# Group mean, values and FFN moved ahead of the query product on TensorE, and the copies issued ahead of the image's load

## The reference

```python
x = x + bn(dwconv(x, dw0_w, 1), dw0_bn)             # x: the image after a group norm (32 groups)
x = ffn(x, ffn0_w1, ffn0_bn1, ffn0_w2, ffn0_bn2)    # x + pw(relu(pw(x)))
x = x + window_attn(x, qkv_w, qkv_bn, qdw_w, qdw_bn, attn_bias, proj_w, proj_bn)
x = x + bn(dwconv(x, dw1_w, 1), dw1_bn)
x = ffn(x, ffn1_w1, ffn1_bn1, ffn1_w2, ffn1_bn2)
...
# window_attn: 25 windows of 7x7 (padded at two edges), 4 heads, 16 channels for queries and keys, 32 for values
q = bn(dwconv(q, qdw_w, 2), qdw_bn)                  # 5x5 depthwise convolution of the queries, per window
attn = softmax(einsum('bhcn,bhcm->bhnm', q, k) * KD ** -0.5 + bias)
out = einsum('bhdm,bhnm->bhdn', v, attn)
return pw(relu(out), proj_w, proj_bn)
```

## Time and profile before

| | before |
|---|---|
| median of 3 runs | 4045.66 us (4044.58 to 4047.29) |
| the profiled execution's own time | 4038.97 us |
| its span, first to last instruction | 4037.1 us |
| TensorE matmul busy | 3184.8 us (79%) |
| VectorE busy | 2720.9 us (67%) |
| ScalarE busy | 2203.4 us (55%) |
| mean granted TensorE clock | 0.889 of full speed |

### The profile page before, as it was taken

The page is one execution under the profiler, slowest core; times in us unless marked ns, Lnnn a source line. Parts: engine busy times, 40 slices in busy tenths (PEclk is TensorE's granted clock), DMA queues, the critical chain, the costliest instruction groups (busy, mean ns, idle before and its releaser), DMA issues. The chain is left out here.

```text
span 4037.1 us, 80272 instructions
## 1 busy us (share of the span) xinstructions
PE 3184.8 (79%) x29652; PEld 2441.9 (60%) x29652; DVE 2720.9 (67%) x5162; ACT 2203.4 (55%) x3568; POOL 743.2 (18%) x869
## 2 busy tenths in 40 slices
PE   4787878787846658888888888888888886699993
PEld 2444445454535546767766777676767675587872
DVE  4767676767544448777777777777777775577763
ACT  2444454545524437666666666666656663477760
POOL 1000000000000000122122121121221122466660
PEclk9898999999967779989899888899889997899995
DMA  2344444445437689999999999999999994577768
GB/s 55 108 159 115 155 118 152 122 148 164 131 134 271 246 285 375 342 333 343 345 352 347 329 346 332 347 351 336 337 337 336 366 334 151 187 243 236 242 201 334
DMA packets 291012, 1023.89 MB, mean 254 GB/s; under 512 B 51620, under 2 KB 57520, under 8 KB 281574
## 3 DMA queue, kind: packets, MB, share of 16 engines
q1 hardware_dynamic: 273382, 985.62, 70.5%
q0 software_dynamic: 17280, 33.87, 2.3%
HBM read 486.25 MB, written 489.85 MB: 242 GB/s over the span
## 5 line engine op out<-in xcount | busy, mean ns | idle before, releaser
L1094 DVE CUSTOM_DVE_ANT_0 att_skewed<-att_score_ps,att_skewed 128x1024 f32<-128x1024 f32 x512 | 625.2, 1221 | 260.1 <-issue 243.2
L956 ACT ACTIVATE att_skewed<-att_skewed,att_neg_max 128x1024 f32<-128x1024 f32 x512 | 588.8, 1150 | 347.9 <-DVE att_neg_max L1094 347.0
L1212 PE MATMUL att_turn_ps<-att_ident,att_skewed 128*128 128x128 f32 x4096 | 592.0, 291 | 112.7 <-ACT att_skewed L956 110.4
L947 ACT ACTIVATE att_rows<-att_wide_ps 128x1152 f32<-128x1152 f32 x512 | 574.1, 1121 | 176.3 <-PE att_wide_ps L1176 174.9
L1212 PEld LDWEIGHTS att_turn_ps<-att_ident,att_skewed 128*128 128x128 f32 x4096 | 494.7, 149 | 280.3 <-ACT att_skewed L956 242.1
L1102 DVE COPY att_turned<-att_turn_ps 128x1024 f32<-128x1024 f32 x512 | 625.0, 1221 | 27.7 <-PE att_turn_ps L1212 27.4
L1176 PE MATMUL att_wide_ps<-att_ps,att_qs 98*128 98x128 f32 (+3 forms) x1920 | 452.9, 359 | 53.9 <-issue 29.6
L1204 PE MATMUL att_score_ps<-att_ks,att_qs 96*128 96x512 f32 x1024 | 379.7, 454 | 19.4 <-DVE att_neg_max L1094 17.9
L911 POOL DMA_INDIRECT expert_rows<-att_expert_rows,att_place x256 | 247.1, 965 | 786.6 <-DVE att_place L1052 701.2
L1176 PEld LDWEIGHTS att_wide_ps<-att_ps,att_qs 98*128 98x128 f32 x1920 | 324.5, 209 | 109.2 <-issue 67.7
L152 POOL DMA_INDIRECT expert_parts<-exp_parts,exp_rows x284 | 301.4, 1061 | 192.3 <-ACT exp_parts L183 126.3
(11 more groups left out here) (257 smaller groups left out, 5586.5 us busy)
## 6 DMA issues: line engine op xcount, KB each, us to landing
skewed_rows<-att_rows SPq DMA_DIRECT2D x512, 576.0 KB, 5.5
att_skewed<-skewed_rows SPq DMA_DIRECT2D x512, 512.0 KB, 6.9
expert_rows<-conv_pad SPq DMA_DIRECT2D x144, 520.0 KB, 10.9
exp_weights<-split_weights SPq DMA_DIRECT2D x71, 1028.0 KB, 7.0
att_qs<-queries SPq DMA_DIRECT2D x192, 128.0 KB
att_ks<-keys SPq DMA_DIRECT2D x192, 128.0 KB
exp_rows<-expert_rows SPq DMA_DIRECT2D x71, 260.0 KB, 2.8
sum_part<-expert_parts SPq DMA_DIRECT2D x32, 512.0 KB, 9.6
```

The source lines that it names most:

```text
L947: act.activation(rows[s % ROWS][:], wide_ps[:, 0:WIDE], ACT.Copy).then_inc(wide_read, 1)
L956: act.activation(skewed[r % RING][:], skewed[r % RING][:], ACT.Exp, bias=neg_max[:, k:k + 1], scale=-1.0, accum_out=sums[:, k:k + 1]).then ...
L1094: dve.tensor_tensor_reduce(skewed[r % RING][:], score_ps[:], skewed[r % RING][:], -SCALE, 3.0e38, ALU.add, ALU.min, neg_max[:, k:k + 1]).t ...
L1212: last = pe.transpose(turn_ps[:, t * P:(t + 1) * P], skewed[r % RING][:, t * P:(t + 1) * P], ident[:])
```

## The change

On TensorE the turn becomes: scores, group mean, first part of the values, first half of FFN 1 (both hidden halves), second part of the values, FFN 1's output, queries, transposes and the rest as before. Of the convolution's four chunks the fourth goes between the hidden halves and the output of FFN 0. The tile rotation (`main_items`, `first_items`) follows this order. ScalarE's order is adapted: values, relu, first exponential, relu, values, windows, second exponential, queries; and the fourth chunk of the convolution is read after FFN 0's relus. On SyncE `copies(n + 1)` comes ahead of the wait for `xp_ready` and the load of image n + 3. VectorE's and GpSimd's programs keep their order; of VectorE's only the tiles differ.

```diff
-        main_items = [*((item, 0) for item in S_ITEMS + ["V0", "V1"]), ("Q", 1), ("G", 2), *((item, -1) for item in F1),
-                      *((item, 0) for item in T_ITEMS + ["A0", "A1", "P0", "P1"]), *((item, 1) for item in ["K0", "K1"] + C_ITEMS),
-                      *((item, 2) for item in F0)]
+        main_items = [*((item, 0) for item in S_ITEMS), ("G", 2), ("V0", 0), ("F1a", -1), ("F1b", -1), ("V1", 0), ("F1c", -1), ("Q", 1),
+                      *((item, 0) for item in T_ITEMS + ["A0", "A1", "P0", "P1"]), *((item, 1) for item in ["K0", "K1"] + C_ITEMS[:3]),
+                      ("F0a", 2), ("F0b", 2), ("C3", 1), ("F0c", 2)]
...
             def turn(n):
+                if not is_last(n):
+                    copies(n + 1)
                 if not (isinstance(n, int) and n >= NB - 3):
                     sp.wait_ge(xp_ready, n + 3)
                     sp.dma_start(x[:], x_dram[n + 3]).then_inc(x_loaded, 16)
-                if not is_last(n):
-                    copies(n + 1)
...
             def turn(n):
...
+                values_of(n, 0)
+                if not is_first(n):
+                    ffn(n - 1, 1, y, "a")
+                exponentials(n, 0)
+                if not is_first(n):
+                    ffn(n - 1, 1, y, "b")
+                values_of(n, 1)
                 if not is_last(n):
                     into_windows(n + 1)
-                exponentials(n, 0)
+                exponentials(n, 1)
                 if not is_last(n):
                     queries(n + 1)
-                exponentials(n, 1)
                 if not is_first(n):
-                    ffn1(n - 1)
+                    filled(act, place(n - 1, "F1c"))
...
                     keys_of(n + 1)
-                    convolved(n + 1)
+                    convolved(n + 1, (0, 1, 2))
                     keep_branch(n + 1)
                 if has_after_next(n):
                     ffn0(n + 2)
+                if not is_last(n):
+                    convolved(n + 1, (3,))
...
+            def prepare(n):
+                convolution(n, (0, 1, 2))
+                if not is_last(n):
+                    pe.wait_ge(x1_ready, n + 2)
+                    ffn_in(n + 1, 0, x1)
+                convolution(n, (3,))
+                if not is_last(n):
+                    ffn_out(n + 1, 0)
...
             def turn(n):
...
+                if has_after_next(n):
+                    moments_mean(n + 2)
+                values_of(n, 0)
+                if not is_first(n):
+                    pe.wait_ge(x4_ready, n)
+                    ffn_in(n - 1, 1, x4)
+                values_of(n, 1)
+                if not is_first(n):
+                    ffn_out(n - 1, 1)
                 if not is_last(n):
                     queries(n + 1)
-                if has_after_next(n):
-                    moments_mean(n + 2)
-                if not is_first(n):
-                    ffn1(n - 1)
...
                 if not is_last(n):
                     keys_of(n + 1)
-                    convolution(n + 1)
-                if has_after_next(n):
-                    ffn0(n + 2)
+                    prepare(n + 1)
```

More of the change, by code:

```diff
@@ L1538, in ffn0, with values_of @@
                 ffn(n, 0, branch, "ab")
-            def ffn1(n):
-                ffn(n, 1, y, "ab")
-                filled(act, place(n, "F1c"))
+            def values_of(n, v):
+                at = place(n, f"V{v}")
+                filled(act, at)
+                first, k = 16 * v, min(16, WINDOWS - 16 * v)
+                for low in range(2):
+                    rows = slice(64 * low, 64 * low + WIN)
+                    source = tile[at[0]][rows, 0:k * 64].rearrange("p (w a d) -> p w a d", w=k, a=2)
+                    ins = act.activation(values[rows, first:first + k, :, low * DH:(low + 1) * DH], source, ACT.Copy)
+                ins.then_inc(tile_used[at[0]], 1)
             def queries(n):
@@ L1561, in keys_of, with convolved @@
                                        last=(h == HEADS - 1 and s > 0))
-            def convolved(n):
-                for j in range(4):
+            def convolved(n, chunks):
+                for j in chunks:
                     at = place(n, f"C{j}")
@@ L1623, in prologue @@
                 keys_of(0)
-                convolved(0)
+                convolved(0, (0, 1, 2))
                 keep_branch(0)
                 ffn0(1)
-            image_loop(act, prologue, turn, lambda: ffn1(NB - 1))
+                convolved(0, (3,))
+            image_loop(act, prologue, turn, lambda: ffn(NB - 1, 1, y, "ab"))
         @block.vector
@@ L1834, in begin, with ffn_in @@
                 return tile[where[0]]
-            def ffn(n, number, source):
+            def ffn_in(n, number, source):
                 for j in range(2):
@@ L1842, in ffn, with ffn_out @@
                     last.then_inc(tile_filled[at[0]], 1)
+            def ffn_out(n, number):
                 at = place(n, f"F{number}c")
@@ L1889, in keys_of, with convolution @@
                     last.then_inc(tile_filled[at[0]], 1)
-            def convolution(n):
-                pe.wait_ge(copied, 256 * n + 256)
-                for j in range(4):
+            def convolution(n, chunks):
+                if 0 in chunks:
+                    pe.wait_ge(copied, 256 * n + 256)
+                for j in chunks:
                     at = place(n, f"C{j}")
@@ L1907, in prologue, with values_of @@
                 moments_mean(1)
-                ffn0(0)
+                pe.wait_ge(x1_ready, 1)
+                ffn_in(0, 0, x1)
+                ffn_out(0, 0)
                 queries(0)
                 keys_of(0)
-                convolution(0)
-                ffn0(1)
+                prepare(0)
+            def prepare(n):
[6 more added lines that the diff above has]
+                    ffn_out(n + 1, 0)
+            def values_of(n, v):
+                at = place(n, f"V{v}")
+                to = begin(at)
+                for j in range(min(16, WINDOWS - 16 * v)):
+                    for low in range(2):
+                        last = pe.matmul(to[64 * low:64 * low + WIN, 64 * j:64 * j + 64], xw[:, 16 * v + j, :], w_v[:, low, :], start=True, stop=True)
+                last.then_inc(tile_filled[at[0]], 1)
             def turn(n):
@@ L1929, in turn @@
                     last.then_inc(tile_filled[at[0]], 1)
[L1930 to L1934, removed]
-                            last = pe.matmul(to[64 * low:64 * low + WIN, 64 * j:64 * j + 64], xw[:, 16 * v + j, :], w_v[:, low, :], start=True, stop=True)
-                    last.then_inc(tile_filled[at[0]], 1)
+                if has_after_next(n):
[7 more added lines that the diff above has]
+                    ffn_out(n - 1, 1)
                 if not is_last(n):
                     queries(n + 1)
-                if has_after_next(n):
-                    moments_mean(n + 2)
-                if not is_first(n):
-                    ffn1(n - 1)
                 for j in range(4):
@@ L1973, in turn, with epilogue @@
                     keys_of(n + 1)
-                    convolution(n + 1)
-                if has_after_next(n):
-                    ffn0(n + 2)
-            image_loop(pe, prologue, turn, lambda: ffn1(NB - 1))
+                    prepare(n + 1)
+            def epilogue():
+                pe.wait_ge(x4_ready, NB)
+                ffn_in(NB - 1, 1, x4)
+                ffn_out(NB - 1, 1)
+            image_loop(pe, prologue, turn, epilogue)
 def tables():
```

17 lines of the change are left out of this document (1 added, 16 removed).

## The result

The changed kernel takes **3936.36 us** (median of 4 runs, 3928.71 to 3939.22), the kernel before 4045.12 us in runs beside it: the ratio is 0.9733, 95% interval 0.9711 to 0.9756. The profiled execution took 3937.88 us with a span of 3935.8. Forecast were 3924 us and a range of 3895 to 3975.

What follows compares the result with a forecast made beforehand. TensorE's order with two late suppliers bounds each turn. Turns 0 to 12 give 113 us, turn 13 1.2, turns 14 and 15 3 each, prologue 0.9: 121 us, so 3918 profiled, 3924 as median; range 3895 to 3975.

Steps and rivals of the forecast that it cites:

- Two late suppliers: On TensorE, the convolution waits for its copies and the query product for the windows, 4.5 to 5 us each turn.
- The first half: Scores to keys on TensorE: queries follow at once and warm, attention starts at 27.1, keys end at 36.8.
- the wait of the values: On TensorE, the values' second part waits 1.8 us for VectorE's copy that releases the group mean's tile.
- the transposes' wait: On TensorE, the third transposes wait 3.1 us, until 24.5, for VectorE to read the FFN's output tile.
- The clock: TensorE's clock falls behind the transposes' 3.1 us wait, costing 1.2 us a turn, bounds 0 and 9.
- Rival 2: Clock falls at the new waits, staying low through attention, projection and keys: 5 us a turn, 3977 us; chance 0.10.
- rival 1: Clock stays high past the 3.1 us wait: turn 57.1 us, bound by copies, 3910 us in all; chance 0.22.
- The copies: On SyncE, issued at 20.7 and landed 15.1 us later at 35.8, just covered; the load behind costs nothing.
- Turn 0: First turn of the convolution phase: said to wait like turns 1 to 12 and to gain the same 8.7 us.
- The exponential between the relus: On ScalarE, the first exponential takes 1.53 us, to 11.9; one table load in the whole phase was noted.
- The second half: Convolution start to next scores takes 21.2 us; the relu wait shrinks from 1.39 to about 0.5 us.
- rival 3: The new TensorE order gains nothing and only the copies help: 98 us gained, 3948 us; chance 0.15.

Runs made afterwards that it cites:

- e1: The kernel before with only SyncE's copies moved ahead of the image's wait and load, old engine order kept: 3956.29 us, ratio 0.9787 to the kernel before.
- e2: The changed kernel with SyncE's old order, the image's load ahead of the copies: 3950.94 us, ratio 0.9774 to the kernel before.
- e10: e3 plus a fourth unread matmul behind the last transposes, in the wait for ScalarE's copy: 3909.34 us, ratio 0.9670 to the kernel before.
- e5: The changed kernel with VectorE's sum moved into a softmax gap and the tile's read ahead of the group norm: 3906.28 us, ratio 0.9669 to the kernel before.
- e9: The program of e3 run once more, unedited, beside the changed kernel: 3923.47 us, ratio 0.9699 to the kernel before.
- e7: e5 with VectorE's copy of the group mean ahead of the two maxima: 3899.37 us, ratio 0.9656 to the kernel before.
- e6: The changed kernel with VectorE's group norm moved behind the sum and the read: 3917.89 us, ratio 0.9696 to the kernel before.
- e3: The changed kernel with three unread matmuls on TensorE filling the wait before the third group of transposes: 3933.26 us, ratio 0.9729 to the kernel before.

## Why the prediction was right, and where it was off

**The bound.** Two late suppliers to an ordered TensorE: right. Each, removed alone (e1, e2), gives most of the gain.

**The first half.** In turn 7 the wait of the values was 1.48 us (1.8 forecast); the queries followed at 17.0 (17.2), warm; the transposes' wait was 3.37 us (3.1) and ended at 24.4 (24.5). The new order's effect was right to 0.3 us at each step.

**The clock.** This is the term that was mis-sized. The direction was right, a fall behind the 3.1 us wait, but I priced it at 1.2 us. With the clock kept high (e10) a turn takes 56.78 us, so the fall costs 2.3 us: in the turn shown the transposes and nearly the whole attention ran at half rate, and the clock rose only with the projection. On average over turns 1 to 12 the attention started at 27.7 (27.1 forecast) and the convolution at 38.0 (36.8). In turn 1 the attention started at 28.2, beyond the 28 that the prediction gave as a sign of being wrong. Rival 2 named the mechanism with 5 us a turn and rival 1 its absence; at 57.1 us a turn rival 1's time was 0.3 from what e10 shows. That the low clock comes every turn was the Trainium skill's reading (TensorE: Matmul & The Clock Gate, HAM oscillation): the trace of the changed kernel agrees in turns 1 to 14, but e5 and e9 have turns with equal waits where it comes and where it doesn't.

**The copies.** In turns 1 to 13 issued at 20.6 (20.7), landed before the keys' end, no wait: right. That 15.1 us from issue to start is the price with nothing ahead is shown by e5 and e7 from turn 2 on. The load behind them cost nothing: no engine waited for it. Turn 0 was wrong. The prediction gave it the gain of the other turns, but its copies took 16.65 us and the convolution waited 4.89 us for them.

**The exponential between the relus.** It loads no table: the changed kernel's trace has one table load in this phase, at 44.2 us, as before, and none in a turn. The query product was due at 17.2 and came at 17.0.

**The second half.** From the convolution at 552.34 to the scores at 573.38 it took 21.0 us, forecast 21.2; the relu's wait was 0.22 us, not 0.5.

**The sum.** Forecast 121 us, found 106.0 in the phase: turns 1 to 12 gave 12 x 7.73 = 92.8 instead of 104; turn 0 5.1 instead of 8.7 (its turn is 60.9 us; e1's is 57.6, where the copies are issued at 16.7 and the convolution doesn't wait); turn 13 0.3 for 1.2; turn 14 3.1 for 3; turn 15 3.65 for 3; the prologue 1.1 for 0.9. So of the 15 us that are missing some 12 lie in turns 1 to 12, where the clock's term was 1.1 us short, and 3.6 in turn 0. The medians differ by 108.8 us; the rest of the program, from the mark to its end, took 2893 to 2908 us over all profiles without a change in its code, so a difference of a few us between phase and median says nothing. Against rival 3 (3948): e1 gives 3956, and the order 16.9 us more in the phase. It was nearly right about what the copies alone bring, and wrong that the order adds nothing. The range's upper end, 3975, was put 2 us below the 3977 of rival 2 that it was meant to reach.

**Open.** What decides whether the clock falls around the transposes: e9 has both outcomes with the same waits. The transposes alone don't do it, since without a wait ahead they left it high (turn 0, and every turn before the change), but no run shows what their light work adds to a wait. Why the copies took 16.65 us in turn 0 and 16.2 in turn 1 of the changed kernel but 15.1 later, and whether they could be made shorter than that, was not tried.

## What to carry to other kernels

Where one engine's order waits for two suppliers, remove each alone before you add their gains: here 89 and 90 us made 106. When work is reordered, a tile reused sooner makes its last reader urgent, so look at what stands in front of that read on the reading engine; moving the two readings was worth another 32 us here (start of the next phase, 1036.6 to 1004.9). A wait on TensorE can cost its own length and what the clock takes behind it; a few matmuls that nobody needs, run in the wait, tell the two apart.

## What the runs showed of the hardware

- The granted clock stayed at 1.00 around the FFN's wait of 1.39 us before and fell behind waits of 2.43 (e6) and 3.37 us (the change) at the transposes. It also fell behind 0.79 and 1.37 us in some turns of one kernel and stayed high in others (e3, e9; likewise behind 1.53 and 1.37 us in e5), and stayed at 1.00 for 502 us once these were 0.79 and 0.51 (e10).
- At the convolution it was 0.50 behind a wait of 4.89 us (turn 0 of the change) and 0.52 behind 1.96 (e5, turn 5), but 1.00 behind 1.84 (e5, turn 7) and behind 2.89 (e5, turn 14). The length of a wait alone didn't decide.
- Behind a wait of 3.37 us the low clock lasted through the whole attention, x100 in the rows (5.57 us for 3.12); the clock was 1.00 again in the convolution.
- Sixteen copies within the core's memory took 15.0 to 15.2 us from the first issue to the start of their reader where it waited for them (e5 and e7, turns 2 to 13), at a DMA share of 1.0 and 196 to 213 GB/s (the change, 538.4 to 548 us). With one image's load ahead in the queue it was 16.6 to 17.1 us (e2, turns 2 to 12).
